# Attention scores on 64 of the 128 contraction rows, two heads side by side on the array

## The chip, the cores and the metric

The kernel runs on one core of a Trainium2 chip. The metric is the time of one execution on the device in microseconds (us), the median of several runs. The core has five engines that run their own instruction streams and meet at semaphores: PE (TensorE, the 128x128 matmul array), DVE (VectorE), ACT (ScalarE), POOL (GpSimd) and SP, whose queue issues most DMAs.

## What is computed

One post-norm transformer layer on x of 4 x 1024 x 256 in float32: attention with 16 heads of 16 dimensions, then a mixture of 16 routed and 2 shared experts. Only the attention is touched:

```python
cond = (jnp.abs(diff) <= WINDOW) & (jnp.abs(diff) % DILATION == 0)   # diff = key index - query index
allowed = jnp.where(cond, 0.0, -jnp.inf)
mask = jnp.maximum(mask, allowed)          # mask was -inf where diff > 0
...
scores = jnp.einsum('bhqd,bhkd->bhqk', q * scale, k) + mask[None, None, :, :]
attn = jax.nn.softmax(scores, axis=-1)
out = jnp.einsum('bhqk,bhkd->bhqd', attn, v)
```

With WINDOW = 64 a query sees every key up to 64 places ahead of it.

## The kernel before

The kernel has three stages: the projections (eight chunks of 512 tokens), the attention, and the experts. The attention works in 16 rounds `G` (4 sequences x 4 groups of `HG` = 4 heads). A score needs more precision than one float16 product gives, so q and k are split into a high and a low half of 16 values each, and one matmul contracts over three blocks of 16 rows (high.high, low.high, high.low), 48 rows for each head. `stack` (lines 331 to 341) writes them from DRAM into `QS` and `KS`: two heads share a `KS` tile, one at partitions 0 to 47 and one at 64 to 111, and `QS` has zeros in the other head's rows, so every score matmul contracts over `MR` = 112 rows.

Each score is computed twice. `scores` (line 561) makes tiles with queries on the partitions, in a unit of one, two or four heads, adds the causal mask to the bank with a second matmul (`idb` x `tri`, 128 columns or fewer, line 575), and DVE takes the row maxima from it (`smax`, line 984). There are `NU` = 45 such units in a round, in `UNITS`, and they go around three PSUM banks: unit u uses bank u % 3 and waits until DVE has finished unit u - 3. `scoresT` (line 580) makes tiles with keys on the partitions, with one row more (the negated maximum), and ACT takes their exponentials (line 863); these use three more banks. POOL zeroes the masked corner, and `weighted` (line 592) multiplies the exponentials with v, four heads side by side in 32-column groups (line 604).

A round has 13 slots (`SLOTS`, a half `qc` of the queries times a tile `kt` of 128 keys). The tensor engine's order in a slot is written out by hand:

```python
for i in range(NSL):
    rest = share(i)
    for h in range(HG):
        scoresT(G, p, k, i, h)
        some_scores(rest[h:h + 1] if h < HG - 1 else ())
    if i:
        weighted(G, p, i - 1)
    some_scores(rest[HG - 1:])
    if i == MAXT[1]:
        maxT(G, 1)
```

`share(i)` hands the units out over the slots. The last `TAIL` = 4 units of a round fall in its slot 0, and from slot 1 on the units are those of the next half or round. `maxT` (line 616) transposes the finished maxima in slots 1 and 9; they go by ACT (`mT_copy`) and one DMA (`put_max`, line 356) into a row of `QS`. `outT` (line 628) transposes the output in slots 2 and 7, and DVE normalises it (`normal`, lines 999 and 1003).

At the start DVE zeroes `QS`, makes the low half of the projection weights (line 969) and sets rows 96 to 127 of `KS` to one (line 975). POOL zeroes `KS` and builds `idb` and `tri`. PE waits for these and for the first x chunk, split by POOL.

Of the kernel before, what the change touches and what calls it, by code (L numbers as in the profile page):

```python
# [31 lines left out]
MR = 112  # L32
# [28 lines left out]
def share(slot):  # L61
# [4 lines left out]
    return [((n - TAIL) % NU, n >= TAIL) for n in range(lo, hi)]  # L66

# [112 lines left out]
def attention_memory(sb):  # L180

    v_all = sb("v_all", [P, NR, S // P, VW], F32)
    QS = [sb(f"QS{p}", [P, NH2, HG, CH], F16) for p in range(2)]
    KS = [sb(f"KS{p}", [P, NH2, HG // 2, CH], F16) for p in range(2)]
    VG = [sb(f"VG{p}", [P, S // P, VW], F32) for p in range(2)]
    idb = sb("idb", [P, P], F16)
    tri = sb("tri", [P, P], F16)
# [6 lines left out]
    return v_all, QS, KS, VG, idb, tri, mx, mT, OTs, rec, raw, PT  # L194
# [17 lines left out]
def program(nc, ctx, banks, ident, proj, att, norms, exps, o_all, wh, wl, q_dram, k_dram, c_dram, x, xT, winT,  # L212
# [13 lines left out]
    v_all, QS, KS, VG, idb, tri, mx, mT, OTs, rec, raw, PT = att  # L226
# [9 lines left out]
    s = sems("""zeroed stack_zero tri_done stack_const otb_zero stacked00 stacked01 stacked10 stacked11  # L236
# [17 lines left out]
    NST = NSL * HG  # L254
    LAST_OF = [max(u for u in range(NST) if u % 3 == n) for n in range(3)]
# [44 lines left out]
    with nc.Block() as block:  # L300

        @block.sync
        def _(sp):
# [22 lines left out]
            def stack(G, p, half):  # L326

                for e in range(2):
                    for dst, src, n, both_at, one_at in ((QS[p], q_dram, HG // 2, 0, 2 * HD),
                                                         (KS[p], k_dram, 0, HD, 0)):  # L330
                        a = src[:, bass.ds(G * (2 * HD) + e * HD, HD), half].rearrange("s d i t -> s d (i t)")
                        to = dst[:, half, n * e:n * e + 2, :].rearrange("p i t -> p (i t)")
# [21 lines left out]
            def put_max(G, p, half):  # L354
                sp.wait_ge(s["mT_done"], G * NH2 + half + 1)
                sp.dma_start(QS[p][MR:MR + 1, half, :, :].rearrange("o h t -> o (h t)"), mT[half][:])\
                  .then_inc(negmax[half][p], 16)
# [10 lines left out]
            sp.wait_ge(s["stack_const"], 4)  # L368
# [81 lines left out]
        def _(pool):  # L450
            pool.memset(idb[:], 0.0).then_inc(s["zeroed"], 1)
            pool.memset(tri[:], 0.0).then_inc(s["zeroed"], 1)
            pool.wait_ge(s["zeroed"], 2)
            pool.affine_select(out=idb[:], in_=idb[:], compare_op=ALU.not_equal, fill=BIG, base=0,
                               pattern=[[-1, P]], channel_multiplier=1).then_inc(s["tri_done"], 1)

            pool.affine_select(out=tri[:], in_=tri[:], compare_op=ALU.is_ge, fill=-BIG, base=0,
                               pattern=[[-1, P]], channel_multiplier=1).then_inc(s["tri_done"], 1)
# [6 lines left out]

# [821 lines left out]
```

## Time and profile before

| | |
|---|---|
| time, median of 3 runs | 1293.54 us (1290.63 to 1294.56) |
| span of the profiled execution | 1287.9 us |
| PE busy | 1214.8 us, 94% |
| DVE busy | 947.5 us, 74% |
| ACT busy | 625.9 us, 49% |
| POOL busy | 238.9 us, 19% |

Of the profiled execution only the span is given, not a time of its own; the span is 5.6 us under the median of the runs, and what lies around it (start and end of the program) is in that difference. "Busy" of PE is modelled: matmuls overlap, each takes longer than the distance to the next, so the distances between starts say more than the durations. The projections fill the first 100 us, the attention the stretch from 100 to about 640 us, and the experts the rest.

### The profile page before, as it was taken

How to read it: one execution, taken by the hardware profiler on the slowest of the kernel's cores; microseconds unless marked ns; L12 is line 12 of the kernel's file. 1: busy time of each engine (PE TensorE's matmuls, PEld its weight loads, DVE VectorE, ACT ScalarE, POOL GpSimd, SP SyncE). 2: the span in 40 equal slices, each digit the busy share in tenths (PEclk: the TensorE clock that was granted, in tenths of full speed). 3: DMA queues.
4: the chain of work that ended last, by engine and by line, in shares of the span. 5: the costliest groups of instructions: out<-in, count | busy, mean ns of one | idle time of the engine just before them, and what ended most of it. 6: DMA issues, size and time to landing. Idle time of an engine off the chain costs nothing.

```text
span 1287.9 us, 28066 instructions
## 1 busy us (share of the span) xinstructions
PE 1214.8 (94%) x8448; PEld 644.6 (50%) x8448; DVE 947.5 (74%) x1975; ACT 625.9 (49%) x1366; POOL 238.9 (19%) x432
## 2 busy tenths in 40 slices
PE   7877999999999999999799999898998989989997
PEld 4543444444444444443356666565665656556564
DVE  7587888888888888887657776676776767757754
ACT  4415777777777777777633332323222232222332
POOL 8831222222222222222401010010200102000000
PEclk9998999999999999999999999898999999999999
DMA  5631111111111111110131232121312212122220
GB/s 166 187 116 53 38 39 39 37 37 37 37 37 37 37 34 32 34 36 14 46 84 61 48 99 59 61 71 43 90 49 63 77 51 90 50 47 77 59 82 33
DMA packets 62443, 76.78 MB, mean 60 GB/s; under 512 B 8992, under 2 KB 37408, under 8 KB 62368
## 3 DMA queue, kind: packets, MB, share of 16 engines
q1 hardware_dynamic: 60736, 72.80, 19.2%
q10 hardware_dynamic: 1632, 3.15, 0.8%
q8 instruction: 27, 0.44, 0.2%
q14 instruction: 48, 0.39, 0.1%
HBM read 62.94 MB, written 12.85 MB: 59 GB/s over the span
## 4 chain that ended last, share of the span: by engine, by line
PE 64%; DVE 13%; issue 9%; ACT 7%; SPq 2%; POOL 2%; DMA 2%; DVEq 0%; ACTq 0%; POOLq 0%
PE bank L759 16%; PE bank L604 11%; PE bank L572 9%; PE bank L587 9%; PE bank L772 9%; DVE hf L1192 3%; DVE sg L1185 3%; ACT hh L947 3%; ACT a_PT L863 3%; PE bank L647 2%; PE bank L575 2%; PE bank L688 1%; PE bank L628 1%; PE bank L651 1%; SPq L324 1%
## 5 line engine op out<-in xcount | busy, mean ns | idle before, releaser
L984 DVE TENSOR_REDUCE a_mx<-bank 128x1 f32<-128x512 f32 (+3 forms) x720 | 401.2, 618 | 73.7 <-PE bank L575 44.6
L863 ACT ACTIVATE a_PT<-bank 128x512 f32<-128x512 f32 (+4 forms) x832 | 357.0, 505 | 138.1 <-PE bank L587 137.5
L587 PE MATMUL bank<-a_QS,a_KS 113*128 113x512 f16 (+4 forms) x832 | 269.6, 331 | 11.4 <-ACT a_PT L863 6.1
L572 PE MATMUL bank<-a_KS,a_QS 112*128 112x512 f16 (+4 forms) x832 | 258.6, 332 | 15.5 <-DVE a_mx L984 8.3
L947 ACT CAST hh<-hf 128x512 f16<-128x512 f32 x144 | 89.0, 618 | 332.5 <-DVE hf L1192 332.5
L509 POOL TENSOR_SCALAR_AFFINE_SELECT a_PT<-a_PT 128x256 f32<-128x256 f32 (+1 forms) x288 | 109.6, 381 | 419.0 <-ACT a_PT L863 418.7
L604 PE MATMUL bank<-a_PT,a_VG 128*17 128x512 f32 (+4 forms) x1664 | 179.7, 504 | 6.4 <-POOL a_PT L509 6.4
L772 PE MATMUL bank<-dh,hh 128*128 128x256 f16 x576 | 159.0, 276 | 16.9 <-DVE z L1207 16.9
L1199 DVE TENSOR_TENSOR hl<-hf,hh 128x512 f16<-128x512 f32 x144 | 99.8, 693 | 99.4 <-ACT hh L947 99.4
L772 PE MATMUL bank<-dh,hl 128*128 128x256 f16 x576 | 159.1, 276 | 0.0
L772 PE MATMUL bank<-dl,hh 128*128 128x256 f16 x576 | 159.1, 276 | 0.0
L572 PEld LDWEIGHTS bank<-a_KS,a_QS 112*128 112x128 f16 x832 | 79.4, 98 | 114.6 <-DVE a_mx L984 84.2
L587 PEld LDWEIGHTS bank<-a_QS,a_KS 113*128 113x128 f16 x832 | 80.0, 98 | 109.4 <-ACT a_PT L863 54.8
L1192 DVE SCALAR_TENSOR_TENSOR hf<-bank,sg 128x512 f32<-128x512 f32 x144 | 99.5, 691 | 42.9 <-issue 28.5
L940 ACT ACTIVATE sg<-bank 128x512 f32<-128x512 f32 x144 | 85.6, 594 | 89.9 <-PE bank L759 89.9
L1185 DVE TENSOR_TENSOR sg<-sg,cb 128x512 f32<-128x512 f32 x128 | 91.0, 711 | 36.7 <-ACT sg L940 31.2
L575 PE MATMUL bank<-a_tri,a_idb 128*128 128x128 f16 (+1 forms) x576 | 111.3, 212 | 0.0
L523 POOL TENSOR_SCALAR ve<-mv 128x4 f32<-128x4 f32 x16 | 6.4, 402 | 545.2 <-DVE mv L1052 545.2
L759 PE MATMUL bank<-x1h,gh 128*128 (+1 forms) x288 | 87.3, 385 | 0.7 <-ACT cT L904 0.7
L759 PE MATMUL bank<-x1h,uh 128*128 (+1 forms) x288 | 86.0, 380 | 1.6 <-DVE hf L1192 1.6
L759 PE MATMUL bank<-x1l,gh 128*128 (+1 forms) x288 | 86.8, 384 | 0.0
L759 PE MATMUL bank<-x1h,gl 128*128 (+1 forms) x288 | 86.2, 381 | 0.0
(134 smaller groups left out, 1438.2 us busy)
## 6 DMA issues: line engine op xcount, KB each, us to landing
cb<-c_dram SPq DMA_DIRECT2D x128, 256.0 KB, 3.3
q_dram<-p_qk SPq DMA_DIRECT2D x32, 128.0 KB, 2.1
k_dram<-p_qk SPq DMA_DIRECT2D x32, 128.0 KB, 2.1
a_QS<-q_dram SPq DMA_DIRECT2D x64, 64.0 KB
a_KS<-k_dram SPq DMA_DIRECT2D x64, 64.0 KB
xb<-x SPq DMA_DIRECT2D x8, 512.0 KB, 3.6
out<-oo SPq DMA_DIRECT2D x8, 512.0 KB, 4.2
p_xf<-xT ACTq DMA_DIRECT2D x6, 512.0 KB, 4.2
```

Of the source, the lines that this page charges most:

```text
L509: pool.affine_select(out=a, in_=a, compare_op=ALU.is_ge, fill=0.0, base=q0 - (kt * P - WIN), pattern=[[0, 2], [1, w]], channel_multiplier= ...
L572: mm = pe.matmul(bank[:, at:at + hi - lo], QS[p][0:MR, t // NT, h, t % NT * P:t % NT * P + P], KS[p][0:MR, piece, h % 2, 0:hi - lo], start ...
L575: mm = pe.matmul(bank[:, at + m0 - lo:at + hi - lo], idb[:], tri[:, m0 - P * t - WIN:m1 - P * t - WIN], start=False, stop=True)
L587: pe.matmul(stbank[u % 3][:, 0:(qc + 1) * CH - q0], KS[p][0:MR + 1, kt // NT, h % 2, kt % NT * P:kt % NT * P + P], QS[p][0:MR + 1, qc, h, ...
L604: mm = pe.matmul(otbank[32 * h:32 * h + HD + 1, q0 - qc * CH:CH], VG[p][:, kt, h:VW:HG], PT[(p + i) % 2][:, h, 0:(qc + 1) * CH - q0], star ...
L759: mm = pe.matmul(bank[:], ww[:, k, n, :], xx[:, k, bass.ds(t * CH, CH)], start=(i == 0), stop=(i == 5))
L772: mm = pe.matmul(y, a[n % NHB][:, j * P:j * P + P], w[:, n, :], start=(n == 0 and i == 0 and j % 2 == 0), stop=(n == NX - 1 and i == 2), s ...
L863: act.activation(PT[(p + i) % 2][:, h, 0:w], stbank[u % 3][:, 0:w], ACT.Exp)\
L947: act.copy(hh[n % NHB][:], hf[n % 2][:]).then_inc(f["hi_done"], 1)
L984: dve.tensor_reduce(mx[:, piece, t // NT, heads[0]:heads[0] + n, t % NT], sbank[u % 3][:, 0:n * w].rearrange("p (h k) -> p h k", h=n), AX. ...
L1185: dve.tensor_tensor(sg[n % 2][:], sg[n % 2][:], cb[e % NCB][:], op=ALU.mult)\
L1192: dve.scalar_tensor_tensor(hf[n % 2][:], ubank[n % 2][:], 1.0 / WSC, sg[n % 2][:], op0=ALU.mult, op1=ALU.mult).then_inc(f["h_done"], 1)
```

## The change

Each head now contracts over its own 48 rows (49 with the maximum), at partitions 0 to 48 or 64 to 112 (`lane`), and `QS` keeps two heads in the two halves of the partitions instead of zeros. The maximum goes to two rows, by two DMAs. The mask matmuls contract over 64 rows, so a mask of 128 columns takes two (128 and 64 columns). The heads of the units and of the exponentials are reordered, so that a neighbour in the program mostly lies on the other half of the rows. Units of 64 columns now hold two heads and not four, so `NU` is 46.

```diff
-                n = {1: 1, 2: 2, 3: 2}.get(CH // (hi - lo), HG)
-                units += [(t, piece, lo, hi, range(h, h + n)) for h in range(0, HG, n)]
+                firsts = (2, 0) if CH // (hi - lo) > 1 else (2, 0, 3, 1)
+                n = HG // len(firsts)
+                units += [(t, piece, lo, hi, range(h, h + n)) for h in firsts]
...
+def heads_of(slot):
+
+    units = share(slot)
+    first = UNITS[units[0][0]][4][0] if units else HG // 2
+    return (0, 2, 1, 3) if first >= HG // 2 else (2, 0, 3, 1)
...
+def lane(h):
+
+    return 64 * (h // 2)
...
-                wait(pe, s["max_done"], G * NU + u - 2)
+                wait(pe, s["max_done"], G * NU + (u - 2 if u >= 3 else LAST_MAX[u] - NU + 1))
...
-                    mm = pe.matmul(bank[:, at:at + hi - lo], QS[p][0:MR, t // NT, h, t % NT * P:t % NT * P + P],
-                                   KS[p][0:MR, piece, h % 2, 0:hi - lo], start=True, stop=(m1 <= m0))
-                    if m1 > m0:
-                        mm = pe.matmul(bank[:, at + m0 - lo:at + hi - lo], idb[:],
-                                       tri[:, m0 - P * t - WIN:m1 - P * t - WIN], start=False, stop=True)
+                    r, c0, c1 = lane(h), m0 - P * t - WIN, m1 - P * t - WIN
+                    mm = pe.matmul(bank[:, at:at + hi - lo], QS[p][r:r + KR, t // NT, h % 2, t % NT * P:t % NT * P + P],
+                                   KS[p][r:r + KR, piece, h % 2, 0:hi - lo], start=True, stop=(m1 <= m0))
+                    for part in range(2):
+                        f0 = max(c0, 64 * part)
+                        if c1 > f0:
+                            mm = pe.matmul(bank[:, at + f0 - c0 + m0 - lo:at + hi - lo], idb[r:r + 64, part, :],
+                                           tri[r:r + 64, part, f0:c1], start=False, stop=(part == 1 or c1 <= 64))
...
-            pe.wait_ge(s["tri_done"], 2)
+            pe.wait_ge(s["tri_done"], 9)
...
-            for a in (QS[0], QS[1]):
-                dve.memset(a[:], 0.0).then_inc(s["stack_zero"], 1)
...
-            dve.wait_ge(s["stack_zero"], 4)
             for a in KS:
-                dve.memset(a[96:P], 1.0).then_inc(s["stack_const"], 2)
+                for r in (32, 96):
+                    dve.memset(a[r:r + 32], 1.0).then_inc(s["stack_const"], 1)
+            dve.wait_ge(s["tri_done"], 8)
+            dve.tensor_copy(tri[64:P], late[64:P]).then_inc(s["tri_done"], 1)
```

In DVE's program at the start (`p_winl` is the low half of the projection weights, `p_qk` the first cast of a projection) stood before:

```order
L966 MEMSET a_QS 128x2048 x2
L969 SCALAR_TENSOR_TENSOR p_winl<-p_stage,p_winh 128x768 [waits p_w_hi] x2
L975 MEMSET a_KS 32x2048 [waits a_stack_zero,p_b_loaded]
L975 MEMSET a_KS 32x2048
L1022 CAST p_qk<-p_qkf 128x512 [waits p_qk_f32] x4
```

and stands now:

```order
L1000 SCALAR_TENSOR_TENSOR p_winl<-p_stage,p_winh 128x768 [waits p_w_hi] x2
L1006 MEMSET a_KS 32x2048 [waits p_b_loaded]
L1006 MEMSET a_KS 32x2048 x3
L1008 COPY a_tri<-a_late 64x256 [waits a_tri_done]
L1055 CAST p_qk<-p_qkf 128x512 [waits p_qk_f32] x4
```

The four memsets and the copy now stand behind the weights, and the copy raises the ninth count of `tri_done`, for which the first matmul of the program waits:

```order
L680 MATMUL bank<-p_xh,p_winh 128x512 [waits a_tri_done,p_x_split,p_ident_done,p_w_hi]
```

In PE's program of slot 1 (`a_KS,a_QS` with L572 is a unit of scores, `a_QS,a_KS` with L587 a transposed score, `a_tri` the mask, `a_PT` the weighted sum, `ident,a_mx` the transposed maxima) the end of the slot read before:

```order
L572 MATMUL bank<-a_KS,a_QS 128x320 [waits a_max_done]
L575 MATMUL bank<-a_tri,a_idb 128x128
L587 MATMUL bank<-a_QS,a_KS 128x448 [waits a_exp_done]
L604 MATMUL bank<-a_PT,a_VG 17x512 [waits a_masked,a_ot_done,a_v_copied]
L604 MATMUL bank<-a_PT,a_VG 17x512 x3
L616 MATMUL bank<-ident,a_mx 16x128 [waits a_mT_done,a_both_max]
```

and reads now:

```order
L601 MATMUL bank<-a_KS,a_QS 128x320 [waits a_max_done]
L606 MATMUL bank<-a_tri,a_idb 128x128
L606 MATMUL bank<-a_tri,a_idb 128x64
L619 MATMUL bank<-a_QS,a_KS 128x448 [waits a_exp_done]
L637 MATMUL bank<-a_PT,a_VG 17x512 [waits a_masked,a_ot_done,a_v_copied]
L637 MATMUL bank<-a_PT,a_VG 17x512 x3
L601 MATMUL bank<-a_KS,a_QS 128x320 [waits a_max_done]
L606 MATMUL bank<-a_tri,a_idb 128x128
L606 MATMUL bank<-a_tri,a_idb 128x64
L649 MATMUL bank<-ident,a_mx 16x128 [waits a_mT_done,a_both_max]
```

A fourth unit has moved into the slot, behind the weighted sum and directly ahead of the transposed maxima, which wait for it.

## Rows read from the trace of the kernel before

**Rows 1.** The page, busy time (us, share of the span, instructions) of each engine.

```profile
span 1287.9 us, 28066 instructions
PE 1214.8 (94%) x8448; PEld 644.6 (50%) x8448; DVE 947.5 (74%) x1975; ACT 625.9 (49%) x1366; POOL 238.9 (19%) x432
```

**Rows 2.** Busy time in three stretches: round 0's start, one middle round, the last round.

```profile
core 0: us, PE busy (x) PEld busy (x) DVE busy (x) ACT busy (x) POOL busy (x), PEclk, DMA share, GB/s
101.00:111.70 10.70, 5.84 (x28) 2.43 (x26) 3.87 (x8) 4.11 (x9) 1.31 (x4) 0.53 0.25 69
564.93:597.76 32.83, 32.39 (x255) 13.86 (x254) 27.48 (x60) 24.29 (x59) 7.33 (x20) 1.00 0.11 33
605.56:640.00 34.44, 29.05 (x225) 12.16 (x221) 18.66 (x58) 26.42 (x66) 11.80 (x23) 1.00 0.14 43
```

**Rows 3.** Timeline of PE where one round ends and the next begins.

```profile
start us, us, engine line op out<-in xcount [idle before <-releaser]
571.20 0.75 PE L604 MATMUL bank<-a_PT,a_VG 128*17 128x320 f32 x8
572.26 0.53 PE L604 MATMUL bank<-a_PT,a_VG 128*17 128x192 f32 x8 [0.31 <-POOL a_PT L509]
572.73 0.39 PE L587 MATMUL bank<-a_QS,a_KS 113*128 113x512 f16 x1
572.95 0.38 PE L572 MATMUL bank<-a_KS,a_QS 112*128 112x512 f16 x1
573.17 0.19 PE L575 MATMUL bank<-a_tri,a_idb 128*128 128x64 f16 x1
573.21 0.38 PE L587 MATMUL bank<-a_QS,a_KS 113*128 113x512 f16 x1
```

**Rows 4.** Timeline of DVE through the same middle round, the rows that begin with idle time.

```profile
565.13 2.42 DVE L984 TENSOR_REDUCE a_mx<-bank 128x1 f32<-128x512 f32 x4 [0.84 <-PE bank L572]
568.05 2.28 DVE L984 TENSOR_REDUCE a_mx<-bank 128x1 f32<-128x448 f32 x4 [0.50 <-PE bank L575]
570.62 1.89 DVE L984 TENSOR_REDUCE a_mx<-bank 128x1 f32<-128x512 f32 x3 [0.28 <-PE bank L572]
573.40 3.81 DVE L984 TENSOR_REDUCE a_mx<-bank 128x1 f32<-128x512 f32 x7 [0.90 <-PE bank L575]
...
578.14 1.29 DVE L984 TENSOR_REDUCE a_mx<-bank 128x1 f32<-128x320 f32 x3 [0.84 <-PE bank L575]
580.43 0.26 DVE L999 RECIPROCAL a_rec<-bank 128x16 f32<-128x16 f32 x1 [1.00 <-PE bank L628]
...
591.91 0.69 DVE L984 TENSOR_REDUCE a_mx<-bank 128x1 f32<-128x512 f32 x1 [0.76 <-PE bank L572]
```

**Rows 5.** Timeline of DVE, then of PE, then of POOL, at the start.

```profile
6.33 3.73 DVE L969 SCALAR_TENSOR_TENSOR p_winl<-p_stage,p_winh 128x768 f16<-128x768 f32 x2 [1.12 <-ACT p_winh L819]
10.55 1.76 DVE L975 MEMSET a_KS<- 32x2048 f16 x1 [0.48 <-issue]
12.69 1.76 DVE L975 MEMSET a_KS<- 32x2048 f16 x1 [0.38 <-issue]
...
8.53 1.01 PE L647 MATMUL bank<-p_xh,p_winh 128*128 128x512 f16 x2 [8.53 <-POOL p_xl L472]
...
14.99 4.98 POOL L479 TENSOR_TENSOR p_qk<-p_qkf,p_qk 128x512 f16<-128x512 f32 x4 [2.62 <-DVE p_qk L1022]
```

**Rows 6.** Timeline of PE: the transposed maxima of slot 1 in rounds 0 and 15.

```profile
111.73 0.28 PE L616 MATMUL bank<-ident,a_mx 128*16 128x128 f32 x1
...
610.33 0.28 PE L616 MATMUL bank<-ident,a_mx 128*16 128x128 f32 x1
```

**Rows 7.** Groups of instructions by shape between 200 and 500 us.

```profile
L984 DVE TENSOR_REDUCE a_mx<-bank 128x1 f32<-128x512 f32 x218 | 138.8, 683 | 26.5 <-PE bank L572 17.9 <-PE bank L575 8.6
L863 ACT ACTIVATE a_PT<-bank 128x512 f32<-128x512 f32 x216 | 111.7, 608 | 39.5 <-PE bank L587 39.5
```

**Rows 8.** DMA issues from 100 to 600 us: size and median us to landing.

```profile
a_QS<-a_mT SPq DMA_DIRECT2D x30, 4.0 KB, 2.8
```

More of the change, by code:

```diff
@@ L66, in share @@
     return [((n - TAIL) % NU, n >= TAIL) for n in range(lo, hi)]
+def heads_of(slot):
+    units = share(slot)
+    first = UNITS[units[0][0]][4][0] if units else HG // 2
+    return (0, 2, 1, 3) if first >= HG // 2 else (2, 0, 3, 1)
+HEADS = [heads_of(i) for i in range(NSL)]
+def lane(h):
+    return 64 * (h // 2)
 def settle(eng, sem):
@@ L182, in attention_memory @@
     v_all = sb("v_all", [P, NR, S // P, VW], F32)
-    QS = [sb(f"QS{p}", [P, NH2, HG, CH], F16) for p in range(2)]
+    QS = [sb(f"QS{p}", [P, NH2, HG // 2, CH], F16) for p in range(2)]
     KS = [sb(f"KS{p}", [P, NH2, HG // 2, CH], F16) for p in range(2)]
     VG = [sb(f"VG{p}", [P, S // P, VW], F32) for p in range(2)]
-    idb = sb("idb", [P, P], F16)
-    tri = sb("tri", [P, P], F16)
+    idb = sb("idb", [P, 2, P], F16)
+    tri = sb("tri", [P, 2, P], F16)
+    late = sb("late", [P, 2, P], F16)
     mx = sb("mx", [P, 2, NH2, HG, NT], F32)
@@ L254, in program @@
     NST = NSL * HG
+    LAST_MAX = [max(u for u in range(NU) if u % 3 == n) for n in range(3)]
     LAST_OF = [max(u for u in range(NST) if u % 3 == n) for n in range(3)]
@@ L355, in put_max @@
                 sp.wait_ge(s["mT_done"], G * NH2 + half + 1)
-                sp.dma_start(QS[p][MR:MR + 1, half, :, :].rearrange("o h t -> o (h t)"), mT[half][:])\
-                  .then_inc(negmax[half][p], 16)
+                for e in range(2):
+                    at, n = 64 * e + KR, HG // 2 * NT
+                    sp.dma_start(QS[p][at:at + 1, half, :, :].rearrange("o i t -> o (i t)"),
+                                 mT[half][n * e:n * e + n]).then_inc(negmax[half][p], 16)
             project(0, 0, 0)
@@ L602, in weighted @@
                     pe.wait_ge(s["exp_done"], G * NST + (i + 1) * HG)
-                for h in range(HG):
+                for n, h in enumerate(HEADS[i]):
                     mm = pe.matmul(otbank[32 * h:32 * h + HD + 1, q0 - qc * CH:CH], VG[p][:, kt, h:VW:HG],
-                                   PT[(p + i) % 2][:, h, 0:(qc + 1) * CH - q0], start=(kt == 0),
+                                   PT[(p + i) % 2][:, n, 0:(qc + 1) * CH - q0], start=(kt == 0),
                                    stop=(i in HALF), skip_group_check=True)
@@ L727, in body @@
                     rest = share(i)
-                    for h in range(HG):
-                        scoresT(G, p, k, i, h)
-                        some_scores(rest[h:h + 1] if h < HG - 1 else ())
+                    for n in range(HG):
+                        scoresT(G, p, k, i, n)
+                        some_scores(rest[n:n + 1] if n < HG - 1 else ())
                     if i:
@@ L829, in mT_copy @@
                 if not (isinstance(G, int) and G == 0):
[L830 removed]
+                    act.wait_ge(negmax[half][1 - p], (k + p) * 32)
                 act.mul(mT[half][:], aux[0:HG * NT, 0:P], -1.0).then_inc(s["mT_done"], 1)
@@ L907, in body @@
                 for i in range(NSL):
-                    for h in range(HG):
-                        exp(G, p, i, h)
+                    for n in range(HG):
+                        exp(G, p, i, n)
                     if i == 0 and not (isinstance(G, int) and G == 0):
```

67 lines of the change are left out of this document (38 added, 29 removed).

## The prediction

> **What bounds the kernel now.** I read the page first: PE is busy for 94% of the span, DVE for 74%, ACT for half [rows 1]. A share over the whole program does not say which engine sets the attention's pace, so I next took one middle round by itself, from the transposed maxima of one round to those of the next, 32.83 us [rows 2]. PE is busy for 32.39 of them, DVE for 27.48, ACT for 24.29, all at the full clock. The reader is to see two things there: PE sets the pace, and DVE is only 5.35 us behind it. Then the timeline of DVE through that round shows where these 5.35 us lie: seven gaps of 0.84, 0.50, 0.28, 0.90, 0.84, 1.00 and 0.76 us, all ended by PE [rows 4], 5.12 us in sum.
>
> The change touches 15 rounds of the 16. In the last one no units for a later round are left: it holds only transposed scores and weighted sums and the first norm's steps, with DVE at 18.66 and PE at 29.05 of 34.44 us [rows 2]. Round 0 is only reached after a wait for a DMA, in which the clock stood at 0.53 of full [rows 2], and PE arriving earlier there waits longer. So the rate counts from the mark at 111.73 to the one at 610.33 us, 498.6 us or 15 rounds [rows 6]. Projections and experts keep their instructions.
>
> **What it removes from PE.** A score matmul of 512 columns starts 0.22 us after the one before (572.73, 572.95), and the next one 0.26 us later with a 64-column mask between them [rows 3]. A round has 52 transposed scores with 20,224 columns, as many columns in the units, and 3,840 in masks: 44,288 columns at 512 in 0.22 us are 19.0 us. Behind the change the two kinds alternate between the halves of the rows. If a matmul may start as soon as the one ahead has started and its own half is free, I get, walking down the new order slot by slot, 13.1 us in place of 18.8 (the columns of the longer of each pair, plus masks, now 5,632 columns, that mostly stand alone). That is 5.7 us less PE work a round, from about 31.5 to 25.8 us with the weighted sums (1.06 us from 571.20 to 572.26 with a wait inside, for 320 columns) as they are [rows 3]. No row of this kernel shows two matmuls on different row halves at once. The nearest is the weighted sum, where eight float32 matmuls of 192 columns fill 0.47 us (572.26 to 572.73), 0.06 us each [rows 3]: the 64-column float16 mask needs 0.04, so 192 columns with float32's passes could not fit unless the four column groups ran together. I take full overlap, and keep none at all for the other end.
>
> **What DVE then allows.** PE's 25.8 us is under DVE's 27.48. So DVE is the next bound, and the round is DVE's work plus the gaps that PE still leaves it. The work grows by one small reduction: 27.6 us. The gaps I took one by one, with three banks ahead of DVE, 0.60 us for each full reduction back to back (four in 2.42 us, each 0.68 long) [rows 4, 7], and about 0.2 us from the end of a matmul's streaming to DVE's start (mask at 573.17 plus 0.03, DVE at 573.40) [rows 3, 4]:
>
> - Round seam, 0.90 now. Two weighted sums stand in a row there, the second waiting for POOL [rows 3], 2.15 us without a unit; DVE now comes with full banks (1.8 us). About 0.5 stays.
> - Unit 0. 45 units divide by the three banks, 46 do not. Unit 0 now follows unit 45 on the same bank and waits until DVE has emptied all three: DVE idles for PE's answer, two heads of 192 columns and their masks (0.33 us) and 0.2, so about 0.55. New.
> - Slot 1, 0.84 now. Unit 3 has moved behind the weighted sum of 1.0 us, while units 0 to 2 give DVE only 1.3 us of work: about 0.7 idle. Then the transposed maxima wait for DVE itself, and the next unit comes 0.55 us after. Together 1.25 for 0.84.
> - Normalisation in slot 2, 1.00 now: DVE waits for the transposed output behind a weighted sum; unchanged, 1.0. Slot 7, 0.76 now: about 0.45, ahead of the unit behind the weighted sum.
> - Slots 9, 10 and 12, 0.84, 0.50 and 0.28 now: about 0.5, 0.15 and 0.1.
>
> That is 4.3 to 4.5 us in place of 5.12. The round comes to 31.9 to 32.1, so 0.7 to 0.9 us less; the walk's other rounding pulls to 0.95. I take 0.93, times 15 is 14 us gained. The Trainium skill says the same of the direction (TensorEngine Tiling, PSUM Bottleneck): tiling speeds up the matmuls but not the emptying of PSUM, which may become the bottleneck. By the factor of up to 2 that this page gives for a contraction of at most 64 rows (Theoretical Speedup), and nothing else in the way, the 19 us would fall to 9.5, and 15 rounds would give back some 140 us, a sum by which the kernel would take about 1160 us; the rows on DVE above forbid it.
>
> **What it adds.** At the start DVE's memsets of `KS` go from two to four and stand ahead of the copy that PE's first matmul waits for. They follow each other at 2.14 us (10.55, 12.69) [rows 5]. Four from 10.5 end at about 18.8, the copy at about 19.0. PE started at 8.53 [rows 5], so it is 10.5 us later. The removed memsets (DVE's of `QS`, POOL's of `KS`) ran ahead of data that arrived later anyway: nothing back. A little returns, since the first POOL split of q and k had itself waited for DVE's memsets (it began at 14.99) [rows 5]: now it begins 8 us later and not 10.5, but the next chunk hangs on PE again; I count 0.6. The projections that follow are a chain from PE over ACT, DVE and POOL to the DMAs, with PE gapless for some 40 us, so 9.9 us stay. Ends: 7.5 if the chain gives POOL's 3 back, 11.
>
> One more reduction where DVE paces the last projection chunks adds 0.3. The maxima's second DMA adds 0.6 us of issue to a path of about 0.9 us up to SP and 2.8 to landing [rows 8]; it has 5.4 us until slot 5 needs it, so it is hidden, by 1 us. If that cover is gone, each round pays what is over. ACT, at 24.29 us, stays under the pace.
>
> **Sum.** 1293.5 + 9.9 + 0.3 - 14 = 1289.7, so 1290 us by the median, 1284 by the span.
>
> **Rivals.**
> - *PE runs well ahead and most gaps close.* Against it stands that two of the gaps are order, not speed. If the walk overstates them and 2 us stay, a round is 29.5, 3.3 less: 50 us gained, 10 lost, 1254. Chance 0.20.
> - *The row halves don't run at once.* PE then carries 1,792 more mask columns, 0.8 us, and the unit-0 wait, 0.5: 1.3 a round, 20 us, and 10 at the start: 1323. It decides as soon as PE's round exceeds 32.83. It is slower than before. For it speaks only that no row shows the overlap. Chance 0.12. The Trainium skill states the overlap plainly (TensorE: Matmul & The Clock Gate, Packing small matmuls), four tiles of 32 rows at 3.07 times the rate; no row here shows it.
> - *The overlap works, the new waits eat all of it.* PE, DVE and ACT are within 4 us of each other, and each stall of PE at a bank of one starves the other. With 0.1 us more at each of seven gaps the gain is 0.2 a round, 3 us, and the start decides: 1300. Chance 0.15.
> - *DVE-bound as worked out*, gain 0.3 to 1.9 a round, 1275 to 1300: chance 0.53.
>
> **Chances.** A measurement of this kernel tells about 0.3% (3.9 us) from no change. Of the likeliest case half lies below 1289.7 (0.26), 0.15 within, 0.12 above 1297.4. With the rivals: faster 0.46, same 0.19, slower 0.35. The range takes in 1254 and what a small part of the serial case gives: 1254 to 1312; the likeliest alone has 1275 to 1300.
>
> **What would show it.** PE's first matmul at 19 us. In a middle round a unit's matmul starting within 0.1 us of the transposed score ahead of it; DVE busy 27.6 of about 31.9 us; PE waiting for DVE's maxima at unit 0 with some 0.5 us idle on DVE behind it, and again at the transposed maxima of slot 1; the round's marks 31.9 us apart. The prediction is wrong if the halves don't overlap, if the delay at the start is made up in the projections, or if the gaps of DVE differ from these by more than 1 us a round.

## The result, and the profile after

The changed kernel takes 1381.86 us, median of 4 runs (1379.21 to 1384.32), against 1292.29 us (1290.63 to 1294.56) for the kernel before in the same comparison: a ratio of 1.0696, with a 95% interval from 1.0669 to 1.0723. It is 7% slower, 92 us above the forecast and far outside its range. The page of the changed kernel answers [rows 1]:

```profile
span 1382.6 us, 29057 instructions
PE 1248.7 (90%) x8896; PEld 633.7 (46%) x8896; DVE 951.5 (69%) x1992; ACT 625.3 (45%) x1366; POOL 236.8 (17%) x437
PEclk9997897898888899788778999999999999999999
```

The last row is TensorE's granted clock over the span, in 40 slices and tenths of full speed. Slices 5 to 20 are the attention, and it reads 7, 8 and 9 there. The forecast had looked at one middle round of before, at 1.00 [rows 2], and took that over. Three windows of the changed kernel (columns as in [rows 2]):

```profile
415.80:437.00 21.20, 17.88 (x176) 7.39 (x175) 16.60 (x34) 12.87 (x37) 6.73 (x18) 1.00 0.17 50
438.20:449.00 10.80, 10.71 (x69) 3.78 (x70) 5.99 (x13) 5.86 (x12) 0.00 (x0) 0.53 0.00 0
140.00:580.00 440.00, 393.82 (x3272) 150.88 (x3269) 324.68 (x708) 280.80 (x683) 83.88 (x221) 0.86 0.11 32
```

The first window is all at 2.4 GHz; in the second the clock is at 1.2 GHz for 10.2 us, and the third is the mean. The stretches at 1.2 GHz last from 3.4 to 17.1 us and come to 168 us in the 15 rounds. Before, not one microsecond of these rounds was granted less than full. PE's timeline shows the price at both levels, in one weighted sum of 512 columns (eight matmuls on all rows, unchanged by the edit), and that the two halves of the rows do run at once:

```profile
408.24 1.07 PE L637 MATMUL bank<-a_PT,a_VG 128*17 128x512 f32 x8
...
410.15 0.39 PE L619 MATMUL bank<-a_QS,a_KS 49*128 49x512 f16 x1
410.16 0.39 PE L601 MATMUL bank<-a_KS,a_QS 48*128 48x512 f16 x1
...
655.84 1.92 PE L637 MATMUL bank<-a_PT,a_VG 128*17 128x512 f32 x8
```

The same eight matmuls fill 1.07 us at the full clock and 1.92 us at the half. L619 and L601 are a transposed score and a unit's score of 512 columns each, and they start 0.01 us apart; before, such a pair was 0.22 us apart [rows 3].

The marks that [rows 6] has for before, the transposed maxima of slot 1 in rounds 0 and 15:

```profile
124.68 0.38 PE L649 MATMUL bank<-ident,a_mx 128*16 128x128 f32 x1 [0.67 <-DVE a_mx L1025]
...
695.78 0.38 PE L649 MATMUL bank<-ident,a_mx 128*16 128x128 f32 x1
```

They divide the 94.7 us by which the span grew. Up to the first mark it is 13.0 us (124.68 for 111.73): the first matmul is 10.5 us later, and a stretch at half clock lasts longer (17.1 us for 10.2). The 15 rounds take 571.1 us for 498.6, so 38.07 us each for 33.24: 72.5 us. The last round and the experts take 9.2 us more, with 0.73 of the clock in the last round's window, 1.00 before [rows 2]:

```profile
695.78:733.00 37.22, 31.89 (x205) 12.11 (x205) 17.62 (x54) 23.00 (x58) 11.67 (x21) 0.73 0.13 40
```

How the 72.5 us divide: each round has two parts, from the mark of slot 1 to that of slot 9 and back. Over these 30 parts the time follows the half clock in each: of the short ones 13.67 us with none and 14.73 with 3.1; of the long ones 21.6 with 3.6, 22.6 with 7.1, 24.7 with 10.2. A straight line through the 15 whole rounds gives 0.39 us lost for each microsecond at half clock and 33.7 us for a round without any. No round of this execution is without, but run 8 below has four, at 33.9 to 34.1. So about 65 us (0.39 x 168) are the clock's and about 7 (0.5 a round) are lost even at full clock, where the forecast had 14 us gained. The line shows that the time goes with the clock; what brought the clock down is for the experiments.

In a stretch at full clock the waits of the forecast can be looked up. PE at the seam and in slots 0 to 5:

```profile
426.60 0.25 PE L601 MATMUL bank<-a_KS,a_QS 48*128 48x192 f16 x1 [1.13 <-DVE a_mx L1017]
...
429.78 0.27 PE L649 MATMUL bank<-ident,a_mx 128*16 128x128 f32 x1 [0.74 <-DVE a_mx L1025]
...
435.43 0.39 PE L619 MATMUL bank<-a_QS,a_KS 49*128 49x512 f16 x1
435.43 0.60 PE L601 MATMUL bank<-a_KS,a_QS 48*128 48x512 f16 x2
...
438.10 0.39 PE L619 MATMUL bank<-a_QS,a_KS 49*128 49x512 f16 x1 [1.67 <-ACT a_PT L896]
```

DVE in the same stretch, the rows that begin with idle time:

```profile
424.06 2.48 DVE L1017 TENSOR_REDUCE a_mx<-bank 128x1 f32<-128x512 f32 x4 [0.86 <-PE bank L606]
427.25 1.42 DVE L1017 TENSOR_REDUCE a_mx<-bank 128x2 f32<-128x384 f32 x3 [0.71 <-PE bank L606]
429.08 0.49 DVE L1017 TENSOR_REDUCE a_mx<-bank 128x1 f32<-128x320 f32 x1 [0.41 <-PE bank L606]
...
430.44 1.42 DVE L1017 TENSOR_REDUCE a_mx<-bank 128x1 f32<-128x320 f32 x3 [0.78 <-PE bank L606]
432.73 0.26 DVE L1032 RECIPROCAL a_rec<-bank 128x16 f32<-128x16 f32 x1 [0.87 <-PE bank L661]
```

Unit 0 waits 1.13 us for DVE and leaves it 0.71 us idle; the unit behind slot 1's weighted sum leaves 0.41, the transposed maxima wait 0.74 for DVE and it then idles 0.78; the normalisation 0.87. That is the walk, place by place, with the sizes off by up to 0.4 us (the seam has 0.86 where 0.5 was forecast, the unit behind the weighted sum 0.41 for 0.7). PE's last row above was in no step: ACT, on which the exponentials hang, stood before a DMA.

```profile
436.53 0.42 ACT L886 ACTIVATE gh<-a_raw 128x256 f32 x1 [1.24 <-DMA a_raw<-dwT]
```

The casts of the expert weights (`a_raw`) wait for their loads, and `load_raw` stands behind `put_max` in SP's program. `put_max` waits for the copied maxima, which the change made later, and now issues two DMAs. Half a microsecond behind PE's wait, at 438.7, the clock fell.

### The profile page after: what moved, and what is told of

Same layout as the page of the kernel before. It is cut to its first block, busy times and chain, and to the rows that moved or that the text cites. A ratio compares the mean times of both kernels' runs of the same rounds, so it can differ in the third digit from the quotient of the medians.

```text
span 1382.6 us, 29057 instructions
## 1 busy us (share of the span) xinstructions
PE 1248.7 (90%) x8896; PEld 633.7 (46%) x8896; DVE 951.5 (69%) x1992; ACT 625.3 (45%) x1366; POOL 236.8 (17%) x437
## 4 chain that ended last, share of the span: by engine, by line
PE 60%; DVE 16%; issue 9%; ACT 8%; SPq 2%; DMA 2%; POOL 1%; DVEq 0%; ACTq 0%; POOLq 0%
PE bank L792 16%; PE bank L637 12%; PE bank L805 8%; PE bank L619 7%; PE bank L601 6%; ACT a_PT L896 3%; DVE a_mx L1017 3%; DVE hf L1225 3%; DVE sg L1218 2%; ACT hh L980 2%; PE bank L680 2%; PE bank L606 2%; PE bank L661 2%; PE bank L721 2%; DMA a_raw<-dwT 1%
## 5 line engine op out<-in xcount | busy, mean ns | idle before, releaser
L1017 DVE TENSOR_REDUCE a_mx<-bank 128x1 f32<-128x512 f32 (+4 forms) x736 | 405.4, 608 | 130.1 <-PE bank L606 77.7
L896 ACT ACTIVATE a_PT<-bank 128x512 f32<-128x512 f32 (+4 forms) x832 | 353.3, 501 | 183.0 <-PE bank L619 180.0
L619 PE MATMUL bank<-a_QS,a_KS 49*128 49x512 f16 (+4 forms) x832 | 245.6, 363 | 33.6 <-ACT a_PT L896 26.8
L601 PE MATMUL bank<-a_KS,a_QS 48*128 48x512 f16 (+4 forms) x832 | 228.4, 364 | 32.7 <-DVE a_mx L1017 27.1
L637 PE MATMUL bank<-a_PT,a_VG 128*17 128x512 f32 (+4 forms) x1664 | 217.0, 598 | 5.9 <-POOL a_PT L537 5.9
L601 PEld LDWEIGHTS bank<-a_KS,a_QS 48*128 48x128 f16 x832 | 66.5, 97 | 174.3 <-DVE a_mx L1017 123.4
L619 PEld LDWEIGHTS bank<-a_QS,a_KS 49*128 49x128 f16 x832 | 73.5, 99 | 132.3 <-ACT a_PT L896 99.1
L606 PE MATMUL bank<-a_tri,a_idb 64*128 64x64 f16 (+1 forms) x1024 | 117.8, 217 | 0.0
L606 PEld LDWEIGHTS bank<-a_tri,a_idb 64*128 64x128 f16 x1024 | 89.5, 105 | 22.6 <-issue 6.4
```

The lines of the kernel that those rows point to most:

```text
L601: mm = pe.matmul(bank[:, at:at + hi - lo], QS[p][r:r + KR, t // NT, h % 2, t % NT * P:t % NT * P + P], KS[p][r:r + KR, piece, h % 2, 0:hi ...
L606: mm = pe.matmul(bank[:, at + f0 - c0 + m0 - lo:at + hi - lo], idb[r:r + 64, part, :], tri[r:r + 64, part, f0:c1], start=False, stop=(part ...
L619: pe.matmul(stbank[u % 3][:, 0:(qc + 1) * CH - q0], KS[p][r:r + KR + 1, kt // NT, h % 2, kt % NT * P:kt % NT * P + P], QS[p][r:r + KR + 1, ...
L637: mm = pe.matmul(otbank[32 * h:32 * h + HD + 1, q0 - qc * CH:CH], VG[p][:, kt, h:VW:HG], PT[(p + i) % 2][:, n, 0:(qc + 1) * CH - q0], star ...
L896: act.activation(PT[(p + i) % 2][:, n, 0:w], stbank[u % 3][:, 0:w], ACT.Exp)\
L1017: dve.tensor_reduce(mx[:, piece, t // NT, heads[0]:heads[0] + n, t % NT], sbank[u % 3][:, 0:n * w].rearrange("p (h k) -> p h k", h=n), AX. ...
```

## The experiments

Each ratio is against runs of the kernel before on the same chip, whose median lay between 1289.85 and 1294.35 us, so times of different runs compare to some 5 us only; "half clock" is the sum of the stretches at 1.2 GHz within the 15 rounds of the profiled execution.

**1. start: the late wait of the projections taken off the first matmul.** PE waits for the ninth count of `tri_done` only ahead of the first unit.

```diff
-            pe.wait_ge(s["tri_done"], 9)
...
+                if isinstance(G, int) and G == 0 and u == 0:
+                    pe.wait_ge(s["tri_done"], 9)
```

> The changed kernel with one wait moved: the first matmul of the program no longer waits for the mask tiles, the first unit of scores does. Both theories of the clock give the same here: PE's first matmul goes back from 19.0 to about 8.5 us, and the whole time falls by 10 us against the changed kernel, to about 1372 us. If the projections had absorbed the delay, it falls by under 3 us.

Measured: 1372.91 us (1372.32 to 1373.52), ratio 1.0608 [1.059, 1.0626], 9 us less than the changed kernel; round 38.01 us, half clock 167 us. The total is as expected and a tenth of the loss, but the profiles divide it otherwise than the forecast had it:

```profile
8.10 1.01 PE L682 MATMUL bank<-p_xh,p_winh 128*128 128x512 f16 x2 [8.10 <-POOL p_xl L500]
...
18.91 3.35 DVE L1056 CAST p_qk<-p_qkf 128x512 f16<-128x512 f32 x4
```

PE starts 10.9 us earlier than in the changed kernel, yet the mark of round 0 comes at 118.71 us, only 6.0 earlier and still 7.0 behind the kernel before. DVE's four memsets still stand ahead of its first casts, which began at 14.48 before. Another 1.0 us came back in the 15 rounds. The remaining 5 us of the 12 by which the span fell lie behind the last mark, where the profiled execution had 19 us less at half clock (40 for 59); no edit was made there.

**2. same_lane: neighbours on the same half of the rows.** The order of heads puts most neighbours in the program on one half, which was to keep them from running at once.

```diff
-                firsts = (2, 0) if CH // (hi - lo) > 1 else (2, 0, 3, 1)
+                firsts = (0, 2) if CH // (hi - lo) > 1 else (0, 1, 2, 3)
...
-    return (0, 2, 1, 3) if first >= HG // 2 else (2, 0, 3, 1)
+    return tuple((first + n) % HG for n in range(HG))
```

> The changed kernel with the heads in the order 0, 1, 2, 3 for units and transposed scores, so that neighbours in PE's program mostly lie on the same 64 rows and can't run at once. Theory A, the clock falls because matmuls of half the rows count for less: it still falls, mean granted clock in the attention under 0.9, and PE, slower as well, gives 1450 us or more. Theory B, the clock falls because the overlap shortens PE's work and leaves it waiting: without overlap PE is busy throughout, the clock is 1.0 in the attention, and the time is what the rival of the prediction said, about 1323 us (1305 to 1340).

Measured: 1401.65 us (1393.1 to 1410.6), ratio 1.0812 [1.0744, 1.0881], half clock 218 us, round 39.74. It is 20 us slower than the changed kernel, as much as 50 us more at half clock cost (0.39 x 50); the clock is 0.82 from 140 to 600 us. Theory A's clock came, but neither expected time, and the edit did not do what it was for: where the order goes over to the other half, matmuls still start together.

```profile
425.30 0.30 PE L601 MATMUL bank<-a_KS,a_QS 48*128 48x320 f16 x1
425.33 0.38 PE L619 MATMUL bank<-a_QS,a_KS 49*128 49x512 f16 x1
```

Over the full-clock parts of the 15 rounds the next matmul starts clearly before a score or mask matmul is through in 30% of cases, against 34% in the changed kernel. So this run says nothing on whether PE loses its clock for being done too early.

**3. before46: the kernel before with 46 units.** Full rows; only the 64-column units hold two heads, and unit 0 follows unit 45 on its bank.

```diff
-                n = {1: 1, 2: 2, 3: 2}.get(CH // (hi - lo), HG)
+                n = {1: 1, 2: 2, 3: 2}.get(CH // (hi - lo), 2)
...
-                wait(pe, s["max_done"], G * NU + u - 2)
+                wait(pe, s["max_done"], G * NU + (u - 2 if u >= 3 else LAST_MAX[u] - NU + 1))
```

> The kernel before with one edit: the units of 64 columns hold two heads, so a round has 46 units, and unit 0 of a round waits on the bank of unit 45. Full rows, no overlap. Theory C, the clock falls because of the new waits (unit 0, transposed maxima behind the fourth unit of slot 1): it falls here too, under 0.95 in the attention, and the time rises by 30 us or more over the kernel before. Theories A and B: the clock stays at 1.0 in the attention and a round costs 0.5 to 1.3 us more, so 1300 to 1313 us.

Measured: 1328.17 us (1326.48 to 1331.64), ratio 1.027 [1.0249, 1.0291]. A window of one round, then PE behind a seam:

```profile
186.74:222.22 35.48, 32.63 (x255) 13.91 (x255) 27.93 (x61) 24.24 (x59) 7.22 (x19) 1.00 0.12 36
```

```profile
289.82 0.26 PE L573 MATMUL bank<-a_KS,a_QS 112*128 112x192 f16 x1 [0.98 <-DVE a_mx L985]
...
293.31 0.28 PE L617 MATMUL bank<-ident,a_mx 128*16 128x128 f32 x1 [0.67 <-DVE a_mx L993]
```

The same two waits as in the changed kernel, at full clock. PE waits 1.65 us in them, and a round takes 2.0 us more (35.2 for 33.24): the edit to the units is a loss of its own, some 30 us, which the half rows have to earn back first. Half clock stays at 4 us, so on full rows these waits do not bring the clock down. The time is what theory C expected, the clock what A and B did.

**4. early: the wait of slot 1 taken away, half rows kept.** On top of start, the transposed maxima of slot 1 and DVE's last step ahead of them stand before the slot's weighted sum and units.

```diff
+                    if i == MAXT[1]:
+                        maxT(G, 1)
                     if i:
                         weighted(G, p, i - 1)
                     some_scores(rest[HG - 1:])
-                    if i == MAXT[1]:
-                        maxT(G, 1)
```

> The kernel 'start' with the transposed maxima of slot 1 moved ahead of the weighted sum, and DVE's last step before them ahead of the units of slot 1. It takes away DVE's and PE's wait there (1.4 us a round) and lets the expert weights be loaded earlier, which took away the wait of up to 1.7 us in slot 5. Theory C: with fewer waits the clock recovers to above 0.95 in the attention and the time falls to 1270 us or less. Theories A and B: PE's work is unchanged, the clock stays between 0.8 and 0.92, and the time falls by 10 to 35 us against 'start', to 1340 to 1362 us.

Measured: 1335.66 us (1334.86 to 1336.42), ratio 1.0317 [1.03, 1.0334]; round 35.57 us, half clock 97 us. The wait ahead of the transposed maxima is gone (10.4 us in the 15 rounds of start), that of unit 0 is as it was (14.9 us), and PE's waits for the exponentials are less (18 us for 23). That gives 37 us back, some 27 of them by 70 us less half clock (0.39 x 70). The clock, 0.92 from 140 to 600 us, is that of theories A and B; the time lies between their range and that of C.

**5. rows_u: the kernel before with half rows in the units alone.** The transposed scores stay on 113 rows, so each pair changes between the two ways of using the array.

```diff
-                    mm = pe.matmul(bank[:, at:at + hi - lo], QS[p][0:MR, t // NT, h, t % NT * P:t % NT * P + P],
-                                   KS[p][0:MR, piece, h % 2, 0:hi - lo], start=True, stop=(m1 <= m0))
+                    r, e = (64 * (h // 2), 64 * (h // 2) + 48) if len(heads) < HG else (0, MR)
+                    mm = pe.matmul(bank[:, at:at + hi - lo], QS[p][r:e, t // NT, h, t % NT * P:t % NT * P + P],
+                                   KS[p][r:e, piece, h % 2, 0:hi - lo], start=True, stop=(m1 <= m0))
```

> The kernel before with one edit: a score matmul of a unit with one or two heads contracts over its own 48 rows instead of 112 (the others were zeros). Transposed scores and masks keep the full rows, 45 units, the order and all waits are as before, so hardly anything can overlap and nothing new waits. Theory A (matmuls on half the rows count for less, and the clock falls for that): the granted clock in the attention falls below 0.95 though PE stays busy all the time, and the time rises by 30 us or more. Theory C (new waits): the clock stays at 1.0 and the time within 10 us of before, unless going between 48 and 112 rows costs PE something, which shows in the distance between starts.

Measured: 1424.41 us (1417.13 to 1430.24), ratio 1.1048 [1.0994, 1.1102]; round 41.54 us at a clock of 1.00. So with about half of the score columns on 48 rows the clock did not fall, against what theory A expected, in a kernel whose PE was busy for 456.30 of the 460 us from 140 to 600.

```profile
403.33 0.39 PE L588 MATMUL bank<-a_QS,a_KS 113*128 113x512 f16 x1
403.65 0.39 PE L573 MATMUL bank<-a_KS,a_QS 48*128 48x512 f16 x1
403.97 0.20 PE L576 MATMUL bank<-a_tri,a_idb 128*128 128x64 f16 x1
```

Starts are 0.32 us apart where [rows 3] has 0.22: each change between 64 and 128 rows costs 0.10 us, in either direction. By the Trainium skill (TensorEngine Tiling, Key Properties) changing the tiling mode drains TensorE; the row agrees, with 0.10 us for each change.

**6 and 7. fill128, fill64: early, with more work for PE.** In eight slots of a round stand four matmuls of 256 columns ahead of the last units, on 128 or on 64 rows; nothing reads their results. They write a bank that others use too, and wait for it (not shown in the cut). Here is the version on 64 rows:

```diff
+                for _ in range(4):
+                    pe.matmul(aux[:, 0:2 * P], idb[0:64, 0, :], tri[0:64].rearrange("p n k -> p (n k)"),
+                              start=True, stop=True)
```

> The kernel 'early' with four more matmuls of 256 columns in each of eight slots, their result thrown away: 3.4 us more work for PE a round at full clock, which 'early' has to spare. These contract over all 128 rows. Theory A: they lift the clock, from 0.92 to 0.97 or more in the attention, and the time falls below 'early' (1335.7) in spite of more work, to 1300 to 1325 us. If the clock does not look at such matmuls, the time rises by 20 us or more.

> As 'fill128', but the added matmuls contract over 64 rows; PE's added time and all waits are the same. Theory A in its strict form (rows count): the clock is lower than in 'fill128' and the time 10 us or more above it. If only PE's busy time counts, the two are equal within 4 us, both in clock and in time.

Measured: fill128 1348.0 us (1343.82 to 1363.04), ratio 1.0481 [1.0409, 1.0552], half clock 22 us; fill64 1340.26 us (1333.38 to 1342.17), ratio 1.0393 [1.0368, 1.0418], half clock 27 us. Either brings the clock back to 0.98 or 0.99 from 140 to 600 us and gains nothing, since the added work costs what the clock returns: rounds without half clock take 36.0 us with 128 rows and 34.8 with 64. The gain of 10 to 35 us that theory A expected of fill128 did not come. That both restore the clock alike does not tell rows from pauses.

**8. raw_first: the weight loads ahead of the maxima's DMAs.** On top of start.

```diff
-                put_max(G, p, 1)
                 load_raw(G + NSH, p)
+                put_max(G, p, 1)
```

> The kernel 'start' with the loads of the expert weights issued ahead of the two DMAs of the maxima of slot 1. Where ACT waited up to 1.5 us for the weights in slot 4 to 5, that wait goes. Theory C: a round loses 1 us or more and some of the clock's falls go with the wait, 15 to 40 us less than 'start' (1372.9). Theory A: 5 to 18 us less, from the wait alone. If the later maxima become the wait in its place (slot 5), no change.

Measured: 1347.93 us (1342.21 to 1350.55), ratio 1.0433 [1.0401, 1.0465], 25 us less than start (23 by the ratios); half clock 116 us. That is in theory C's range. Of the 25 us some 20 are the clock's (51 us less at 0.39). This kernel has whole rounds at full clock, so it shows what the half rows are worth without the clock. One of them, and DVE's idle times in it from slot 6 on:

```profile
490.31:524.19 33.88, 30.29 (x283) 12.25 (x283) 27.89 (x61) 23.99 (x59) 7.22 (x19) 1.00 0.12 35
```

```profile
501.55 2.22 DVE L1018 TENSOR_REDUCE a_mx<-bank 128x1 f32<-128x512 f32 x4 [0.48 <-PE bank L603]
504.39 1.29 DVE L1018 TENSOR_REDUCE a_mx<-bank 128x1 f32<-128x512 f32 x2 [0.61 <-PE bank L603]
...
510.62 2.42 DVE L1018 TENSOR_REDUCE a_mx<-bank 128x1 f32<-128x512 f32 x4 [0.55 <-PE bank L603]
513.58 2.28 DVE L1018 TENSOR_REDUCE a_mx<-bank 128x1 f32<-128x448 f32 x4 [0.53 <-PE bank L608]
```

```profile
497.37 0.39 PE L621 MATMUL bank<-a_QS,a_KS 49*128 49x512 f16 x1 [0.41 <-ACT a_PT L897]
...
499.81 0.39 PE L621 MATMUL bank<-a_QS,a_KS 49*128 49x512 f16 x1 [0.51 <-ACT a_PT L897]
```

33.88 us with DVE busy for 27.89: 6.0 us of gaps where the forecast had 4.4. The two ahead of slot 7's units (0.48 and 0.61) were forecast as 0.45 together. PE had waited for ACT's exponentials twice just before (0.41 and 0.51), so it came to the weighted sum of that slot without a lead.

The rows with idle time are not all of PE's waits. The ends of its matmuls are modelled (0.39 us for one whose successor can start after 0.22), so a short wait leaves no gap. In the slot that starts with the weighted sum at 506.34 three units begin at 507.87, 508.27 and 508.67, each 0.06 us after DVE has ended the reduction of the unit three before it (507.81, 508.21, 508.61). And five slots are as long as before to 0.1 us, from one weighted sum to the next: 2.86, 2.89, 2.62, 2.20 and 2.44 us, where the same slots of [rows 2]'s round took 2.78, 2.89, 2.62, 2.19 and 2.44. There the halves running at once gave nothing, as PE got its work done sooner only to stand at a bank.

**9. lane0: start, with all four heads on the first half.** Heads 2 and 3 repeat the scores of 0 and 1.

```diff
-    return 64 * (h // 2)
+    return 0
```

> The kernel 'start' with every head's scores taken from partitions 0 to 48, so the four heads of a group repeat two of them (the output is not the reference's). All score and mask matmuls now lie on the same 64 rows and none can overlap. PE streams as many columns as 'before46' and 1,792 mask columns a round more, with the same waits at unit 0 and slot 1. Theory A (half-row matmuls count for less): the clock falls all the same, half-clock time in the 15 rounds over 100 us where 'before46' had 4, and the time is 1400 us or more. Theory D (only streaming or busy time counts): the clock stays at 1.0 in the attention and the time is 1330 to 1350 us, 'before46' plus 0.8 us a round.

Measured: 1673.11 us (1666.06 to 1685.25), ratio 1.297 [1.2902, 1.3037]; half clock 761 us of 863 in the 15 rounds. A window of one round, one of a stretch before the clock fell, and PE's timeline where it fell:

```profile
239.57:297.43 57.86, 56.54 (x283) 19.95 (x283) 30.09 (x61) 26.99 (x59) 7.21 (x19) 0.56 0.08 22
303.50:310.00 6.50, 6.27 (x70) 3.01 (x68) 6.09 (x16) 5.84 (x18) 1.40 (x4) 1.00 0.01 2
```

```profile
309.15 0.38 PE L621 MATMUL bank<-a_QS,a_KS 49*128 49x512 f16 x1
309.36 0.38 PE L603 MATMUL bank<-a_KS,a_QS 48*128 48x512 f16 x1
309.97 0.39 PE L621 MATMUL bank<-a_QS,a_KS 49*128 49x512 f16 x1 [0.23 <-ACT a_PT L897]
310.29 1.90 PE L639 MATMUL bank<-a_PT,a_VG 128*17 128x512 f32 x8
```

From 303.5 to 310.0 scores follow each other at 0.22 us, as in before, with 0.23 us of waiting in it; then the weighted sum takes 1.90 us, and the clock stays low for most of the round with PE busy for 56.54 of 57.86 us. Pauses can't be the reason here. before46 has the same units and nearly the same columns one after another, on full rows, with more waiting, and stands at 1.00. What differs in PE's stream is that the score matmuls use 48 or 49 rows of the array and not 112 or 113, and the masks 64 and not 128 (with 1,792 mask columns more a round).

**10 and 11. early48, best2: towards a faster version.** early48 is early with two more units, so that 48 divide by the three banks again; best2 adds two 256-column matmuls on 64 rows in the eight slots.

```diff
-                firsts = (2, 0) if CH // (hi - lo) > 1 else (2, 0, 3, 1)
+                firsts = (2, 0) if CH // (hi - lo) > 1 and t > 0 else (2, 0, 3, 1)
```

> The kernel 'early' with the two units of 2 x 192 columns split into four, so 48 units, which divide by the three banks. The wait of unit 0 for the whole queue of DVE goes (about 1.0 us of PE, 0.5 to 0.7 us of DVE a round), two small reductions are added (0.15 us). At an unchanged share of half clock the time falls by 8 to 15 us under 'early' (1335.7), to 1320 to 1328 us; if the clock gains from the missing wait as well, to 1305. If the bank wait was not the cause of DVE's gap, no change.

> The kernel 'early48' with two added 64-row matmuls of 256 columns in each of eight slots, half as many as in 'fill64', to hold the clock. From the rounds of 'early' without half clock (about 33.0 us), less 0.8 for the bank wait, plus 0.6 for the added work: 32.8 us a round against 33.2 before, so 1285 to 1300 us where the clock holds, and 1310 to 1325 where two fillers are too few for that. It is the version that could beat the kernel before.

Measured: early48 1325.59 us (1320.66 to 1336.32), ratio 1.0238 [1.0199, 1.0277], half clock 144 us (its profiled execution is the slowest of the four); best2 1307.11 us (1302.89 to 1308.47), ratio 1.0111 [1.0086, 1.0137], half clock 47 us. In early48 the wait of unit 0, 14.9 us in the 15 rounds of early, is gone, and the time fell by 10 us, within what was expected. But the clock did not rise with it: 0.923 to 0.939 over the program in the four executions, 0.938 to 0.942 in those of early. best2 lies between its two expected ranges.

**12. best3: best2 with the loads of raw_first.**

> The fastest version so far (48 units, transposed maxima of slot 1 ahead, two 256-column matmuls more in eight slots: 1307.1 us) with the expert weight loads issued ahead of the second DMA of the maxima as well. Moving these loads gave 25 us where the clock fell often (1372.9 to 1347.9 us) and took away ACT's waits for the weights. If this wait still costs here, the round falls by 0.3 to 0.7 us and the kernel comes to 1296 to 1303 us; if the extra matmuls and the 48 units already cover it, it stays at 1307. Faster than the kernel before only if a round falls under 33.24 us, which would take over 0.9 us a round.

Measured: 1309.18 us (1300.23 to 1311.88), ratio 1.0144 [1.0121, 1.0168], half clock 40 us. Not told apart from best2. Its rounds without half clock still take 34.3 us, with the added matmuls in them, and no round without half clock of any version on half rows took less than 33.8 us, against the 33.24 us of before.

**13 and 14. few64, few128: early, with a quarter of the added work.** One matmul of 256 columns in the eight slots.

> The kernel with the earlier maxima (1335.7 us, 97 us of half clock in 15 rounds) plus one matmul of 256 columns on 64 rows in eight slots of a round, a quarter of what stood in the run with four (1340.3 us, 27 us of half clock). If the clock falls because half-row matmuls count for less, a few of them change little: half clock 80 to 97 us, 1330 to 1342 us. If it falls because PE pauses, they close the same pauses as full-row ones: the same half clock as the run with full rows, within 10 us.

> The same single matmul of 256 columns in the same eight slots, on all 128 rows. If rows decide, it restores more of the clock than the 64-row one: half clock 40 to 70 us, and two changes of mode in each of eight slots cost up to 1.6 us a round, so 1335 to 1350 us. If only pauses decide, half clock as with 64 rows within 10 us, and the time 10 to 20 us above it for the changes of mode.

Measured: few64 1347.07 us (1345.16 to 1351.18), ratio 1.0443 [1.0413, 1.0472], half clock 119 us; few128 1341.01 us (1330.73 to 1346.99), ratio 1.0383 [1.033, 1.0436], half clock 72 us. early had 97 us. The same small amount of work takes 25 us of half clock off when it lies on 128 rows, and none when it lies on 64; there it is 22 us more, which no theory had foreseen. The clocks of all four runs of few128 (0.943 to 0.958 over the program) are above all four of few64 (0.931 to 0.934). With lane0 this speaks for the rows, but it is not clean: the matmul on 128 rows also brings two changes of mode in each of eight slots (0.10 us each by rows_u), which keep PE from waiting for as long. Full and half rows filled alike in 6 and 7.

## Why the prediction was wrong

The forecast was 1290 us in a range of 1254 to 1312. Its steps in order:

- **The start (9.9 us): right in size, in part by luck.** The first matmul is at 19.03 us, forecast 19.0, and the mark of round 0 is 13.0 us late. But only 6.0 of these hang on the wait that the forecast named; with it gone, DVE's memsets still held the first casts until 18.91 (14.48 before), and the mark was 7.0 us late.

```profile
16.75 1.76 DVE L1006 MEMSET a_KS<- 32x2048 f16 x1 [0.48 <-issue]
18.55 0.22 DVE L1008 COPY a_tri<-a_late 64x256 f16<-64x256 f16 x1
...
19.03 1.01 PE L680 MATMUL bank<-p_xh,p_winh 128*128 128x512 f16 x2 [19.03 <-DVE a_tri L1008]
```

- **The halves of the rows run at once: right.** Pairs start 0.00 to 0.01 us apart. The overlap that the Trainium skill states (TensorE: Matmul & The Clock Gate, Packing small matmuls) is there; its 3.07 times, for four tiles of 32 rows, no run here shows.
- **PE's work falls, DVE is next: right in kind.** At full clock DVE is busy for 27.89 us of a round, forecast 27.6, and PE waits for it at unit 0 and at the transposed maxima of slot 1 as said. What the forecast took from PE's 32.39 busy of 32.83 us, that PE sets the pace and a round shortens with its work until DVE's is reached, held only in part: five slots are as long as before (run 8).
- **The round comes to 31.9 to 32.1 us: wrong by 1.7 to 1.9 us**, even at full clock (33.7 by the line, 33.88 in a row). It set out from 32.83 us [rows 2], the shortest of the rounds before, of which most take 33.0 to 33.3. The gaps left to DVE are 6.0 us and not 4.4. Of the difference 0.6 lie in slot 7, where PE had waited for ACT; 0.4 in slot 10; 0.2 at unit 0; and DVE's own work is 0.3 longer. The walk counted no wait for ACT and no price for changing the rows around the transposes of the maxima and the output: a unit at 376.76 us, the transposed maxima at 377.08 and the next transposed score at 377.29 are 0.32 and 0.21 us apart, some 0.10 more each than without a change. Six such changes a round would make 0.6 us of PE's time, by estimate; what they cost the round was not tried.
- **Unit 0 and slot 1 at some 0.95 us more than before: right on DVE, but not the price of the edit.** DVE's idle time there is 0.71 and 1.19 us (0.41 + 0.78), 1.06 more than the 0.84 of before. But before46, with the same units on full rows, loses 2.0 us a round. The forecast set these waits off against gains at other places of the same walk, and never asked what the edit costs alone. From 35.2 us in before46 to 33.7 or 33.9 the half rows do gain some 1.4 us a round at full clock, but that doesn't pay for the 2.0.
- **The second DMA of the maxima is hidden: wrong place.** Its own landing is. But the forecast looked only at who needs what it carries, not at what stands behind it in SP's program: the expert weights came 1.24 us late for ACT in slot 5 of the round shown, and ACT held PE for 1.67 us. Not all of it is the second DMA's: before46, with one, had such waits too (4.3 us in its 15 rounds, 5.9 in the changed kernel, 0.9 before), as the maxima themselves are later. raw_first took the loads out from behind both.
- **"All at the full clock": the step that failed.** It was read in the profile of before [rows 2] and carried over as if the edit could not touch it; no rival had it. 65 of the 72.5 us of the rounds are this, and part of the 13.0 at the beginning and of the 9.2 at the end. By lane0 against before46 matmuls on half the rows keep the clock up less than the same ones on all rows. The waits that the change brought cost no clock on full rows (before46, 4 us), but on half rows the two runs that took one away had 70 us (early) and 51 us (raw_first) less half clock than start. Two runs do not fit a simple rule: rows_u stayed at 1.00 with half of its score columns on 48 rows, and early48 lost a wait without gaining clock. The Trainium skill (TensorE: Matmul & The Clock Gate, What's actually happening) lets the clock depend on how busy PE has been. early agrees with this, but lane0, busy for 98% of a round at 0.56, shows that being busy is not enough.

The experiments leave open how much of the 168 us is due to the rows and how much to the waits: no run had half rows without any new wait at the speed of the changed kernel, and none kept the halves from running at once with the result of the changed kernel (same_lane was meant to). Nor was it tried whether the count of rows acts evenly or by a limit. The 9.2 us behind the last mark were read from windows and not tested.

## What to carry to other kernels

Before you shrink PE's work in a kernel where PE is not far ahead of the next engine, ask what the granted clock will do: a change that puts matmuls on fewer rows, above all one that gives PE pauses as well, can take away the clock under which all your prices were read, and that belongs among the rivals with a price (here 0.39 us for each microsecond at half clock). Cost each part of a change alone, too: one that brings a loss by itself, as unit 0 on the bank of the last unit (2.0 us a round), is not paid for by a gain that another engine caps. A row of PE without idle time does not say that PE's own work sets the pace there. And when a DMA is added, read what stands behind it in its queue's program, not only who waits for its data.

## What was new about the hardware

- Score matmuls on 48 or 49 rows, following each other at 0.22 us, did not hold the clock: 1.2 GHz in 761 of 863 us with PE busy for 98% of the window shown; on 112 rows, 1.00 (before46). With the units alone on 48 rows it held as well (rows_u, 1.00).
- Two matmuls on the two halves of the rows start 0.00 to 0.01 us apart, but a change between 64 and 128 rows costs 0.10 us in each direction (0.32 for 0.22 us between starts).
- The clock comes back by added work whose results nobody reads: 97 us of half clock became 27 or 22, at a cost that was no less than the gain (1335.66 us became 1340.26 and 1348.0).
